# Two layers of cross-attention: which transpose shares which accumulator bank, and in what order a turn runs

## What is computed

```python
def _L0_xattn_ref(query, context, w_q, w_kv, w_out, b_out):   # 16 heads of 64
    q = query @ w_q
    k, v = jnp.split(context @ w_kv, 2, axis=-1)
    scores = jnp.einsum('bhqd,bhkd->bhqk', q, k) * SCALE
    attn = jax.nn.softmax(scores, axis=-1)
    out = jnp.einsum('bhqk,bhkd->bhqd', attn, v)
    return out @ w_out + b_out
# _L1_xattn_ref: the same on 124 context rows with low-rank additions to the
# weights, plus a second attention over the last 4 context rows ("image")
x = x + _L0_xattn_ref(_layernorm(x, axis=-1), ctx_768, ...)
x = x + _L0_ffn_ref(_layernorm(x, axis=-1), ...)        # 8 experts
...
x = x + _L1_xattn_ref(_layernorm(x, axis=-1), ctx_768, ...)
x = x + _L1_ffn_ref(_layernorm(x, axis=-1), ...)        # 8 experts
```

## Time and profile before

| what | value |
|---|---|
| median of 3 runs | 756.19 us (755.89 to 756.93) |
| the profiled execution, its own time | 755.75 us |
| its span, first to last instruction | 754.0 us |
| PE, DVE, ACT, POOL busy | 661.1, 399.2, 291.9, 196.9 us |
| mean granted TensorE clock | 0.929 of full speed |
| layer 0: turns 0 to 6, then turn 7 | 138.8 to 246.1 us, to 253.7 us |
| layer 1: turns 0 to 6, then turn 7 | 476 to 589.8 us, to 596.8 us |

### The profile page before, as it was taken

How to read it: one execution, slowest core, us unless ns; L and a number is a source line. 1 busy time by engine, 2 the same in 40 slices (tenths; PEclk the granted TensorE clock), 3 DMA queues, 4 the chain that set the end, 5 groups by cost and what they waited for, 6 DMA issues and landing times. The chain is left out here.

```text
span 754.0 us, 13407 instructions
## 1 busy us (share of the span) xinstructions
PE 661.1 (88%) x5200; PEld 543.8 (72%) x5200; DVE 399.2 (53%) x1053; ACT 291.9 (39%) x586; POOL 196.9 (26%) x280
## 2 busy tenths in 40 slices
PE   3495988899998799997899977899998899999997
PEld 2263557788777688887576656788887788888886
DVE  3449574355555565553566634367556654444443
ACT  2443324444544433322344434444453432323331
POOL 8306142035434600002001020035426511111110
PEclk9755697999999999998899988899999999999999
DMA  7900001000000101000000011000000001111100
GB/s 189 216 1 0 0 0 43 2 1 2 1 1 1 44 21 43 22 1 2 1 2 2 2 48 38 1 2 1 2 1 1 1 1 45 54 53 51 51 2 28
DMA packets 23469, 18.44 MB, mean 24 GB/s; under 512 B 5576, under 2 KB 20208, under 8 KB 23408
## 3 DMA queue, kind: packets, MB, share of 16 engines
q1 hardware_dynamic: 23408, 17.60, 8.4%
HBM read 16.68 MB, written 0.52 MB: 23 GB/s over the span
## 5 line engine op out<-in xcount | busy, mean ns | idle before, releaser
L2181 ACT ACTIVATE sb_ca_kt<-bank 128x512 f32<-128x512 f32 x75 | 44.8, 598 | 120.5 <-PE bank L2092 120.2
L2105 PEld LDWEIGHTS bank<-sb_ff_down,sb_ca_o 128*128 128x128 f32 x768 | 88.1, 192 | 1.2
L2105 PE MATMUL bank<-sb_ff_down,sb_ca_o 128*128 128x128 f32 x768 | 88.5, 275 | 0.0
L2092 PE MATMUL bank<-sb_ff_xt_high,sb_ff_low 128*128 128x512 f32 x192 | 79.0, 411 | 5.0 <-DVE sb_ca_o L2260 2.6
L2260 DVE TENSOR_TENSOR sb_ca_o<-sb_ca_kt,bank 128x512 f32<-128x512 f32 x75 | 51.2, 686 | 56.7 <-ACT sb_ca_kt L2181 56.1
L2092 PE MATMUL bank<-sb_ff_xt_high,sb_ff_high 128*128 128x512 f32 x192 | 76.2, 397 | 0.0
L2092 PE MATMUL bank<-sb_ff_xt_low,sb_ff_high 128*128 128x512 f32 x192 | 76.1, 396 | 0.0
L1075 PE MATMUL bank<-sb_ca_vo,sb_ca_pt 128*128 128x130 f32 (+1 forms) x512 | 69.3, 280 | 4.0 <-DVE sb_ca_o L1333 2.7
L1075 PEld LDWEIGHTS bank<-sb_ca_vo,sb_ca_pt 128*128 128x128 f32 (+1 forms) x512 | 63.8, 190 | 9.5 <-DVE sb_ca_o L1333 5.4
L1291 DVE TENSOR_REDUCE sb_ca_m<-bank 128x4 f32<-128x512 f32 (+1 forms) x64 | 40.6, 677 | 40.6 <-PE bank L1029 40.6
L2267 DVE SCALAR_TENSOR_TENSOR sb_x<-bank,sb_ff_cw,sb_x 128x128 f32<-128x128 f32 x128 | 36.1, 345 | 43.3 <-PE bank L2105 43.3
(11 more groups left out here) (359 smaller groups left out, 1251.4 us busy)
## 6 DMA issues: line engine op xcount, KB each, us to landing
sb_ff_w<-in_L_ffn_w_dram SPq DMA_DIRECT2D x8, 256.0 KB, 2.8
sb_ff_gate_up<-in_L_ffn_w_gate_dram SPq DMA_DIRECT2D x8, 256.0 KB, 2.7
sb_ff_gate_up<-in_L_ffn_w_up_dram SPq DMA_DIRECT2D x8, 256.0 KB, 3.0
sb_ff_down<-in_L_ffn_w_down_dram SPq DMA_DIRECT2D x8, 256.0 KB, 3.8
sb_ff_w<-in_L_ffn_w_dram SPq DMA_DIRECT2D x8, 128.0 KB, 2.9
sb_x<-in_x_dram SPq DMA_DIRECT2D x1, 512.0 KB
sb_c_q<-in_L_xattn_w_q_dram SPq DMA_DIRECT2D x1, 512.0 KB, 4.7
sb_c_o<-in_L_xattn_w_out_dram SPq DMA_DIRECT2D x1, 512.0 KB, 7.7
```

What stands on the lines that cost most here:

```text
L2092: mm = nc.tensor.matmul(ps[k % BK][:, :], wp[p][:, g, t * P:(t + 1) * P], xs[xp][:, cols], start=(q == 0), stop=(q == 2))
L2105: mm = nc.tensor.matmul(y_ps[n][:, b * D:(b + 1) * D], h[n][:, t, b * P:(b + 1) * P], down[p][:, t, :], start=(t == 0), stop=(t == FT - 1))
L2181: nc.scalar.activation(s[i % BK][:, :], gate_ps[i % BK][:, :], ACT.Silu).then_inc(act_done, 1)
```

## The change

Three edits, in both layers.

1. The feed-forward's transpose leaves bank 1 and the end of the turn. It follows `x_transpose` at once and writes columns 128 to 255 of the same bank 0; the pair counts as one use, since only its second transpose raises `proj_ready`, and ACT raises `proj_read` after all three copies. Where there is no x to transpose (turns 5, 6 and 7) the feed-forward's transpose stands in that place alone.
2. `max_transpose` is issued behind head group 3 instead of in front of it.
3. On DVE, `normalise(j, 0)` goes in front of `split_max`, and the feed-forward's `vector_apply` in front of groups 1 and 2.

```diff
-            if j >= 2:
-                turn.append(("f", j - 2, 1))
+            if j >= 2 and j + 3 >= NB:
+                turn.insert(6, ("f", j - 2, 0))
...
+        for j in range(2, NB - 3):
+            count["f", j - 2, 0] = count["x", j + 3, 0]
...
             def x_transpose(n):
-                free_bank(("x", n, 0))
-                pe.wait_ge(xn_ready, n + 1)
-                nc.tensor.transpose(proj[0][:, 0:P], xn[n % 2][:, :], pg.ident[:, :]).then_inc(proj_ready, 1)
+                if n < NB:
+                    free_bank(("x", n, 0))
+                    pe.wait_ge(xn_ready, n + 1)
+                    mm = nc.tensor.transpose(proj[0][:, 0:P], xn[n % 2][:, :], pg.ident[:, :])
+                    if n < 5:
+                        mm.then_inc(proj_ready, 1)
+                else:
+                    free_bank(("f", n - 5, 0))
+                if n >= 5:
+                    ffn.tensor_transpose(pe, n - 5, proj[0][:, P:2 * P], proj_ready)
...
-                if j + 3 < NB:
-                    x_transpose(j + 3)
+                x_transpose(j + 3)
+                outputs(j, 3)
                 max_transpose(n)
-                outputs(j, 3)
                 outputs(j, 4)
...
-                if j >= 2:
-                    free_bank(("f", j - 2, 1))
-                    ffn.tensor_transpose(pe, j - 2, proj[1][:, 0:P], proj_ready)
...
             def copy_xt(n):
-                act.wait_ge(proj_ready, count["x", n, 0])
-                nc.scalar.copy(xt[n % 2][:, :], proj[0][:, 0:P]).then_inc(proj_read, 1)
+                if n < NB:
+                    act.wait_ge(proj_ready, count["x", n, 0])
+                    ins = nc.scalar.copy(xt[n % 2][:, :], proj[0][:, 0:P])
+                    if n < 5:
+                        ins.then_inc(proj_read, 1)
+                if n >= 5:
+                    ffn.scalar_copy(act, n - 5, proj[0][:, P:2 * P], proj_ready, count["f", n - 5, 0], proj_read)
...
+                normalise(j, 0)
                 split_max(n)
-                for g in range(3):
-                    normalise(j, g)
                 if j >= 2:
                     ffn.vector_apply(dve, j - 2)
+                for g in range(1, 3):
+                    normalise(j, g)
```

More of the change, by code:

```diff
@@ L917, in _ @@
                 if j >= 3:
-                    ffn.gpsimd_low(pool, j - 3, proj_read, count["f", j - 3, 1])
+                    ffn.gpsimd_low(pool, j - 3, proj_read, count["f", j - 3, 0])
                 if layer and j == 4:
@@ L959, in _ @@
             for b in (LAST - 3, LAST - 2):
-                ffn.gpsimd_low(pool, b, proj_read, count["f", b, 1])
+                ffn.gpsimd_low(pool, b, proj_read, count["f", b, 0])
             ffn.gpsimd(pool)
@@ L1161, in _ @@
             scores_t(LAST, 0)
-            free_bank(("f", LAST - 2, 1))
-            ffn.tensor_transpose(pe, LAST - 2, proj[1][:, 0:P], proj_ready)
+            x_transpose(LAST + 3)
             scores_t(LAST, 2)
@@ L1244, in _ @@
                     copy_k(ahead, 1)
-                if j + 3 < NB:
-                    copy_xt(j + 3)
+                copy_xt(j + 3)
                 copy_max(n)
@@ L1253, in _ @@
                     copy_p2(n)
-                if j >= 2:
-                    ffn.scalar_copy(act, j - 2, proj[1][:, 0:P], proj_ready, count["f", j - 2, 1], proj_read)
                 if layer and j == 4:
@@ L1262, in _ @@
             exp(LAST, 1)
-            ffn.scalar_copy(act, LAST - 2, proj[1][:, 0:P], proj_ready, count["f", LAST - 2, 1], proj_read)
+            copy_xt(LAST + 3)
             exp(LAST, 2)
```

## The result

| | before | after |
|---|---|---|
| median of 4 runs each, taken side by side | 756.08 us (755.89 to 756.93) | 738.25 us (737.43 to 739.65) |
| profiled execution, its span | 755.75, 754.0 | 737.43, 735.7 |
| PE, DVE, ACT, POOL busy | 661.1, 399.2, 291.9, 196.9 | 655.8, 393.9, 290.7, 196.9 |
| mean granted TensorE clock | 0.929 | 0.93 |

The ratio is 0.9764, with an interval of 0.9746 to 0.9782: 17.8 us less. The forecast was 13.5 us less (742.6), and its range ended at 739.8. The sign and the mechanism were right, and the size was not.

What follows compares the result with a forecast made beforehand. PE bounds the kernel, and two of its waits on ACT's copies return in the turns. Savings of 7.0 (middles), 3.6 and 2.9 us (ends, layers 0 and 1) make 13.5, giving 742.6 us; 8-in-10 range 739.8 to 747.

Steps and rivals of the forecast that it cites:

- Both waits: PE at the maxima's transpose for ACT's k copy (3.5 us a layer), at the feed-forward's for values (2.7, 2.8): both go.
- the maxima of layer 1 are in time in turns 3 to 5: Layer 1's turn starts: DVE's first two row maxima still ready for PE, with 0.5 us of slack left.
- bank 0 is free in time: Middle of the turn: bank 0's three copies end before the third quarter of values, with 0.36 us of cover.
- The third edit at zero: DVE's new order: later groups and rows stay hidden from PE; zero gain, bounds 0 and -0.1 us a turn.
- The 0.7 us of turn 6 of layer 0: Saving at that turn's end: 0.99 less 0.10 for the maxima's transpose and about 0.15 for weight transposes needing bank 1.
- longer held up at its second row scores by 0.7: Layer 1, turn 6: PE waits there for DVE's row maxima, which move forward little; only 0.15 us booked for turn 5.
- The product still takes 0.79: Layer 1, turn 5: the image softmax's last product on DVE was kept at 0.78 us beside POOL's sum.
- The ends of the turns as such: Feed-forward transpose plus wait cost 0.99 (layer 0) or 0.91 us; without the transpose's 0.26, 0.73 or 0.65 saved.
- The work in this place is 0.26 + 0.26 + 0.10 = 0.62.: Middle of the turn: PE's price for the x, feed-forward's and maxima's transposes, leaving 0.58 us gained there a turn.
- 6 x 0.58: Middle of turns 0 to 5: 3.5 us saved a layer, 7.0 in all, matching the sums of the wait rows.
- Rival B: Granted clock before layer 1's turn 0: one slow stretch (1.8 us) comes or goes, 740.8 or 744.4; chance 0.13.
- denser turns can only help: Clock: activity releases the throttle, so 740.8 is likelier than 744.4; no such gain inside the turns, already at 1.00.

Runs made afterwards that it cites:

- e3: Changed kernel without the third edit (DVE's order as before); 736.46 us, ratio 0.9727.
- e7: Kernel before with the maxima's transpose behind head group 3; in layer 0 the feed-forward's transpose, still at the turn's end, uses bank 0; 746.52 us.
- e4: Changed kernel with the feed-forward's transpose issued twice into the same columns; 739.54 us, ratio 0.977.
- e10: Kernel before with 16 more x transposes in turn 1 of layer 0; 756.16 us, ratio 0.9997.
- e9: Changed kernel with 16 more x transposes in turn 1 of layer 0; 740.12 us, ratio 0.9784.
- e8: Changed kernel run again unchanged, beside its variants on another chip; 737.92 us, ratio 0.9773.
- e5: Changed kernel with the second half of the transposed scores in front of head group 2 instead of behind it; 732.46 us, ratio 0.9696.

## Why the prediction was wrong

**What it got right.** Both waits, the turns that have them, and that nothing takes their place in the turns: the maxima of layer 1 are in time in turns 3 to 5, bank 0 is free in time, DVE bounds nothing new. The third edit at zero (e3). The 0.7 us of turn 6 of layer 0, with the wait of the weight transposes in it, measured 0.72. Turn 6 of layer 1, longer held up at its second row scores by 0.7, went from 5.70 to 6.33 us. Its row scores and the product in front of them, which answer to the earlier trace rows:

```profile
558.95 0.79 DVE L1325 TENSOR_TENSOR sb_ca_s<-sb_ca_s,sb_ca_sum 128x64 f32<-128x64 f32 x1
...
560.38 0.23 PE L1038 MATMUL bank<-sb_ca_kt,sb_ca_qt 64*128 64x124 bf16 x1 [0.25 <-DVE sb_ca_m L1297]
...
560.96 0.40 PE L1038 MATMUL bank<-sb_ca_kt,sb_ca_qt 64*128 64x124 bf16 x7 [0.35 <-DVE sb_ca_m L1297]
```

The product still takes 0.79 beside POOL's sum, as it was booked. The ends of the turns as such were booked at 1.0 us with the moved transpose in it, and measured 1.00.

**The step that failed: "The work in this place is 0.26 + 0.26 + 0.10 = 0.62."** It is 0.11 + 0.11 + 0.06 = 0.28. The 0.26 was read as the step from 185.03 to 185.29, behind a wait of 0.68 us and in front of row scores. Both count: without the wait, the same step is 0.20 in e7, and the transpose costs the turn 0.11. Behind another transpose or in front of group 3 the step itself is 0.11, as the rows of after and of e4 show. The 0.10 of the maxima's transpose stood behind a wait as well. The 0.34 us a turn that this adds to the gain is what was missing:

| turns | saved each | forecast | more, in all |
|---|---|---|---|
| layer 0, 2 to 5 | 1.67 | 1.31 | 1.4 |
| layer 1, 2 to 4 | 1.57 | 1.23 | 1.0 |
| both layers, 0 and 1 | 0.68 | 0.58 | 0.4 |
| layer 0, 6; layer 1, 5 and 6 | 2.40 together | 2.23 | 0.2 |

Turns 0 and 1 give less than 0.77 (0.94 - 0.11 - 0.06), since 0.1 of the wait is left. PE in turn 0 of the changed kernel, where no second transpose fills it:

```profile
149.28 0.28 PE L976 MATMUL bank<-sb_ident,sb_ca_xn 128*128 128x128 f32 x1
149.40 0.84 PE L1084 MATMUL bank<-sb_ca_vo,sb_ca_pt 128*128 128x130 f32 x6
150.12 0.23 PE L1046 MATMUL bank<-sb_ident_bf,sb_ca_nm 128*128 128x128 bf16 x1
150.22 0.57 PE L1084 MATMUL bank<-sb_ca_vo,sb_ca_pt 128*128 128x130 f32 x3
```

From the x transpose to the second part of group 3 it is 0.94 us here and 0.95 in turn 2 (178.26 to 179.21), with a transpose more. Hence the equal turns.

There was a check in the prediction that looked like support and was none: 6 x 0.58 agreed with the 3.5 us that the wait rows add up to. But a listed wait is less than the wait costs. The wait for k was listed at 0.57 and cost 0.77 (0.79 by e10); that for the values 0.68 and 0.91; that for group 2 0.2 and 0.47. The list of the earlier trace rows also ends too early in time. Taken up to 254 us, the view of the kernel before has the fifth wait at the feed-forward's transpose:

```profile
PE bank L1959 <- ACT sb_ca_vo L1186: 3.4, 5, 0.7
```

No record was missing. The forecast counted five turns anyway, so this changed nothing.

**The clock.** Rival B had the sign open and its size at 1.8 us. One stretch went, at 1.5 us, but behind layer 0's turns and not in front of layer 1's, where the prediction looked. The Trainium skill ("TensorE: Matmul & The Clock Gate", What's actually happening) has activity release the clock; the prediction drew from it that denser turns can only help. Whether that holds of the clock in general, no run here shows; the density of the turns is not what decided here: those of e9 are as dense as those of after, and it has the stretch.

**The sum.** 13.5 forecast, 2.9 more in the turns from the mis-sized steps, 1.5 from the clock. The last 0.4 us, in front of layer 0's turns, lie in the start of the kernel, which the change leaves alone: the same changed kernel took 139.6 us there in one profile and 140.39 in the other (e8), so 0.4 is within what one kernel shows.

## What to carry to other kernels

To price one more instruction, compare two stretches that differ in it alone, or read the step between two of its kind (0.11 us here). The step behind a wait (0.26), the step to an instruction of another kind (0.20) and the instruction's own length (0.27) were all about twice as much or more. What a wait costs is not its row either: here 0.2 to 0.3 us came on top of each, so compare a turn that has it with one that has not. And when a bank's copy holds PE up, first try an order or a bank that another copy has already freed.

## What was not expected of the hardware

- A wait of PE cost more than the idle time listed for it: 0.77 for 0.57, 0.91 for 0.68, 0.47 for 0.2, so 0.20 to 0.27 us more at each of three places. The likely reason, not tested, is that the modelled end of a pipelined matmul counts as busy in front of a wait: PE's busy time fell by 0.27 us a turn in e5 with the same matmuls in it.
- 16 transposes of 128x128 f32 issued in a row took 1.75 us from the first start to the next instruction (e9 and e10), 0.11 us each, though one is shown with 0.27 to 0.28 us. In e9 they added 1.63 us to the turn, since about 0.1 us of the wait for k was left to fill.
- With 1.6 us of extra work well ahead of it (e9), a stretch at 1.2 GHz was back, and the part between the layers took another 1.56 us; the span of that profiled execution is 2.7 us longer, since the part in front of the turns was 0.7 shorter (138.92 against 139.6) and the start of layer 1 0.2 longer.
